# Six probability tiles, a split of the row maxima over two engines, and new instruction lists in an attention block

## What is computed

```python
x = x + _layernorm(_L0_attn_ref(_layernorm(x), W_qkv, b_qkv, W_out, b_out))
x = x + _layernorm(_L0_ffn_ref(_layernorm(x), weight, alpha, bias))
# _L0_attn_ref: 16 heads of 8, 4 groups of keys and values
qkv = x @ W_qkv + b_qkv
scores = einsum('bkgsd,bktd->bkgst', q, k) / sqrt(8)
attn = softmax(where(causal, scores, -inf))
y = einsum('bkgst,bktd->bkgsd', attn, v)
return y @ W_out + b_out
# _L0_ffn_ref: weights become +1, 0, -1 by 0.7 * mean(|w|), times alpha, plus bias
```

## Time and profile before

| | us |
|---|---|
| median of 3 runs (lowest, highest) | 456.02 (455.45, 457.24) |
| the profiled execution | 456.64 |
| its span, first to last instruction | 454.8 |
| busy: TensorE / VectorE / ScalarE / GpSimd | 398.6 / 394.7 / 333.3 / 296.3 |
| TensorE weight loads busy | 280.8 |

### The profile page before, as it was taken

The page is one execution under the profiler, slowest core; times in us unless marked ns, Lnnn a source line. Parts: engine busy times, 40 slices in busy tenths (PEclk is TensorE's granted clock), DMA queues, the critical chain, the costliest instruction groups (busy, mean ns, idle before and its releaser), DMA issues.

```text
span 454.8 us, 19223 instructions
## 1 busy us (share of the span) xinstructions
PE 398.6 (88%) x7430; PEld 280.8 (62%) x7430; DVE 394.7 (87%) x1180; ACT 333.3 (73%) x609; POOL 296.3 (65%) x552
## 2 busy tenths in 40 slices
PE   0569999999999999999999999999999999998551
PEld 0336766676666676666666666676676777764330
DVE  5957878999999999999999999999999989995442
ACT  0333877777888888888888888888888888888332
POOL 2622323657677877777777777787777666766676
PEclk9999999999999999999999999999999999999855
DMA  7176465524434344444344444443444543421342
GB/s 190 35 121 94 103 107 133 127 75 85 77 72 80 81 76 81 78 76 79 66 70 77 76 72 80 81 75 80 82 74 85 114 84 69 87 77 30 111 145 73
DMA packets 72307, 39.59 MB, mean 87 GB/s; under 512 B 13048, under 2 KB 68056, under 8 KB 72216
## 3 DMA queue, kind: packets, MB, share of 16 engines
q1 hardware_dynamic: 70880, 37.70, 41.7%
q10 hardware_dynamic: 1336, 0.66, 0.5%
HBM read 13.67 MB, written 4.72 MB: 40 GB/s over the span
## 4 chain that ended last, share of the span: by engine, by line
PE 47%; DVE 29%; issue 9%; DMA 4%; POOL 3%; SPq 3%; ACT 2%; POOLq 0%; DVEq 0%; ACTq 0%
DVE M L619 13%; PE ps_mx L843 13%; PE ps_y L816 11%; PE ps_w L872 7%; PE ps_st L792 7%; PE ps_w L913 5%; DVE stats L584 4%; DVE xn L602 3%; DMA QS<-part 3%; DVE A L666 2%; DVE mv L594 2%; PE ps_w L893 2%; DVE Mp L683 2%; DVE F L674 2%; SPq L260 2%
## 5 line engine op out<-in xcount | busy, mean ns | idle before, releaser
L619 DVE TENSOR_REDUCE M<-ps_mx 128x2 f32<-128x512 f32 (+3 forms) x352 | 210.5, 626 | 14.2 <-PE ps_mx L843 13.5
L419 ACT ACTIVATE PT<-ps_st 128x1024 f32<-128x1024 f32 (+1 forms) x192 | 165.3, 884 | 20.4 <-PE ps_st L792 20.3
L843 PE MATMUL ps_mx<-KS,QS 112*64 112x128 bf16 (+2 forms) x2560 | 132.7, 228 | 15.9 <-DVE M L619 11.6
L843 PEld LDWEIGHTS ps_mx<-KS,QS 112*64 112x64 bf16 x2560 | 89.6, 112 | 60.9 <-DVE M L619 37.2
L358 POOL TENSOR_TENSOR rstd<-vareps,mhalf 128x2 f32<-128x2 f32 x128 | 93.0, 727 | 10.0
L792 PE MATMUL ps_st<-QS,KS 114*64 114x256 bf16 (+1 forms) x1024 | 97.9, 300 | 0.2 <-DMA QS<-MpT 0.2
L816 PE MATMUL ps_y<-PT,VB 128*32 128x256 f32 (+3 forms) x2048 | 90.4, 304 | 1.3 <-ACT PT L419 1.0
L356 POOL TENSOR_TENSOR vareps<-mv,eps 128x2 f32<-128x2 f32 x128 | 25.9, 203 | 73.3 <-DVE mv L594 73.3
L816 PEld LDWEIGHTS ps_y<-PT,VB 128*32 128x32 f32 x2048 | 46.7, 109 | 28.6 <-issue 9.4
L393 POOL TENSOR_TENSOR rest<-QK,part 128x512 f32<-128x512 f32 x32 | 38.2, 1193 | 24.3 <-ACT part L448 24.1
L792 PEld LDWEIGHTS ps_st<-QS,KS 114*64 114x64 bf16 x1024 | 52.0, 111 | 1.5 <-DMA QS<-MpT 0.5
(11 more groups left out here) (63 smaller groups left out, 512.9 us busy)
## 6 DMA issues: line engine op xcount, KB each, us to landing
QS<-part SPq DMA_DIRECT2D x192, 64.0 KB
rden<-rec_dram SPq DMA_DIRECT2D x32, 256.0 KB
X<-in_x SPq DMA_DIRECT2D x7, 512.0 KB, 6.3
out<-X SPq DMA_DIRECT2D x7, 512.0 KB, 5.4
KS<-part SPq DMA_DIRECT2D x32, 96.0 KB
KS<-part SPq DMA_DIRECT2D x32, 64.0 KB
KS<-part SPq DMA_DIRECT2D x32, 32.0 KB
QS<-MpT SPq DMA_DIRECT2D x32, 16.0 KB
```

Source lines behind the costliest of these rows:

```text
L419: nc.scalar.activation(PT[(b * CHUNKS + n) % TILES][:, 0:512 * banks], ps_st[n % 2][:, 0:banks, :].rearrange("p a c -> p (a c)"), ACT.Exp, ...
L619: nc.vector.tensor_reduce(M[b % 2][:].rearrange("p k g i -> p (k g) i")[:, 2 * kv:2 * kv + pairs, i], ps_mx[(b * BANKS + n) % 2][:, 0:pair ...
L843: last = pe.matmul(ps_mx[(b * BANKS + n) % 2][64 * one:64 * one + 64, at:at + w], q[:, h, BL * i:BL * i + BL], k[:, kv, blocks, :], start= ...
```

## The change

Three things. TILES goes from 3 to 6, so that exp waits for pv of six chunks earlier. `split_max` becomes `high_max`, a single tensor_reduce over an axis of length one that turns M into its high bf16 part, and `low_max` on GpSimd subtracts it from M; the turn waits for both as before. And every list is written in another order, with other distances between the stages: op stands five steps after x1, not six, and the nine stack transfers of a batch are spread over two steps of SP. The lists that run before the loops (on TensorE and VectorE) are changed to match; they are left out below.

```diff
 BANKS = 11
-TILES = 3
+TILES = 6
...
                 load_x(t)
+                spread_rec(t - 5)
+                send_max(t - 3)
+                q_rows(t - 1, 1, 1)
+                q_rows(t - 1, 1, 5)
+                k_rows(t - 1, 2)
+                q_rows(t - 1, 2, 0)
+                store_x(t - 21)
+                send_den(t - 4)
                 rows_free(t)
-                k_rows(t, 0)
+                q_rows(t, 0, 2)
                 q_rows(t, 0, 3)
                 q_rows(t, 0, 4)
-                store_x(t - 25)
+                store_rec(t - 4)
+                k_rows(t, 0)
                 k_rows(t, 1)
-                send_max(t - 2)
-                q_rows(t, 1, 1)
...
                     gp.tensor_tensor(yn[i][:], Y[i][:], rden[i][:], ALU.mult).then_inc(s_yn, 1)
 
+            def low_max(b):
+                if on(b):
+
+                    gp.wait_ge(s_mp, 2 * b + 1)
+                    gp.tensor_tensor(Mp[:, 1, :], M[b % 2][:].rearrange("p k g i -> p (k g i)"), Mp[:, 0, :],
+                                     ALU.subtract).then_inc(s_mp, 1)
...
 
             def step(t):
-                add_normed(t - 10, A2, s_a2, s_x1)
-                third(t - 4)
                 inverse(t, 0)
-                divide(t - 9)
-                inverse(t - 10, 2)
-                inverse(t - 12, 3)
-                inverse(t - 9, 1)
+                divide(t - 8)
                 remainder(t - 3)
-                add_normed(t - 13, F2, s_f2, s_fin)
-
-            for t in range(B + 13):
+                inverse(t - 9, 2)
+                add_normed(t - 12, F2, s_f2, s_fin)
+                low_max(t - 5)
+                inverse(t - 8, 1)
+                third(t - 3)
+                inverse(t - 10, 3)
+                add_normed(t - 8, A2, s_a2, s_x1)
+
+            for t in range(B + 12):
...
             def step(t):
-                take_v(t - 1)
-                exp(t - 4, 3)
-                take_turned(t - 3)
                 take_xn1(t)
-                exp(t - 4, 4)
                 exp(t - 4, 5)
                 take_qk(t)
+                take_y(t - 4)
+                take_xn3(t - 7)
                 first_part(t)
-                take_y(t - 4)
-                norm(t - 10, 3, F1, F2, s_f2, s_fin)
                 exp(t - 3, 0)
+                take_v(t)
                 exp(t - 3, 1)
-                norm(t - 6, 1, A1, A2, s_a2, s_x1)
-                take_xn3(t - 7)
                 exp(t - 3, 2)
+                norm(t - 8, 3, F1, F2, s_f2, s_fin)
                 second_part(t)
-
-            for t in range(B + 10):
+                exp(t - 3, 3)
+                exp(t - 3, 4)
+                take_turned(t - 2)
+                norm(t - 5, 1, A1, A2, s_a2, s_x1)
+
...
@@ -674,15 +682,13 @@
                     nc.vector.tensor_tensor(F1[b % 2][:], ps_w[:, 0:S].rearrange("p (j d) -> p j d", j=TT),
                                             bf_sb[:], ALU.add).then_inc(s_f1, 1)
 
-            def split_max(b):
-                if on(b):
-                    m = M[b % 2][:].rearrange("p k g i -> p (k g i)")
+            def high_max(b):
+                if on(b):
 
                     dve.wait_ge(s_mx, BANKS * b + BANKS)
                     free(dve, b, s_mt_ps)
-                    nc.vector.tensor_tensor(Mp[:, 0, :], m, m, ALU.max).then_inc(s_mp, 1)
-                    dve.wait_ge(s_mp, 2 * b + 1)
-                    nc.vector.tensor_tensor(Mp[:, 1, :], m, Mp[:, 0, :], ALU.subtract).then_inc(s_mp, 1)
+                    nc.vector.tensor_reduce(Mp[:, 0, :], M[b % 2][:].rearrange("p k g i -> p (k g i)").unsqueeze(2), AX_X,
+                                            ALU.max).then_inc(s_mp, 1)
 
...
 
             def step(t):
-                invert_den(t - 10)
-                maxima(t - 7, 4)
-                spread_x1(t - 12)
-                moments(t - 12, 2)
-                moments(t - 14, 3)
-                maxima(t - 7, 5)
-                maxima(t - 7, 6)
-                take_a(t - 11)
-                spread_a(t - 11)
-                moments(t - 11, 1)
-                maxima(t - 7, 7)
-                take_f(t - 13)
-                norm_x1(t - 12)
-                maxima(t - 7, 8)
-                maxima(t - 7, 9)
-                maxima(t - 7, 10)
-                split_max(t - 7)
-                moments(t - 1, 0)
+                maxima(t - 6, 2)
+                norm_x1(t - 11)
+                maxima(t - 6, 3)
+                maxima(t - 6, 4)
+                spread_x1(t - 10)
+                maxima(t - 6, 5)
+                maxima(t - 6, 6)
+                maxima(t - 6, 7)
+                moments(t - 10, 2)
+                maxima(t - 6, 8)
+                maxima(t - 6, 9)
+                invert_den(t - 8)
+                take_a(t - 9)
+                maxima(t - 6, 10)
+                spread_a(t - 9)
+                high_max(t - 6)
+                moments(t - 9, 1)
+                take_f(t - 11)
                 spread_x(t)
-                maxima(t - 6, 0)
-                maxima(t - 6, 1)
-                spread_f(t - 13)
-                maxima(t - 6, 2)
-                norm_x(t - 2)
-                maxima(t - 6, 3)
+                spread_f(t - 11)
+                moments(t, 0)
+                maxima(t - 5, 0)
+                maxima(t - 5, 1)
+                norm_x(t - 1)
...
 
             def step(t):
-                st(t - 4, 4)
+                ff(t - 8)
+                mx(t - 2, 1)
+                pv(t - 4, 0)
+                turn(t - 3)
+                pv(t - 4, 1)
+                pv(t - 4, 2)
+                pv(t - 4, 3)
                 x1(t)
+                mx(t - 2, 2)
+                st(t - 4, 5)
                 mx(t - 2, 3)
-                st(t - 4, 5)
+                qk(t)
                 mx(t - 2, 4)
-                qk(t)
-                mx(t - 2, 5)
-                pv(t - 4, 3)
                 pv(t - 4, 4)
                 pv(t - 4, 5)
+                x3(t - 7)
+                mx(t - 2, 5)
+                st(t - 3, 0)
                 mx(t - 2, 6)
-                op(t - 6)
-                st(t - 3, 0)
+                v(t)
                 mx(t - 2, 7)
-                ff(t - 8)
                 st(t - 3, 1)
                 mx(t - 2, 8)
+                st(t - 3, 2)
                 mx(t - 2, 9)
-                pv(t - 3, 0)
-                x3(t - 7)
+                op(t - 5)
                 mx(t - 2, 10)
-                st(t - 3, 2)
                 st(t - 3, 3)
-                v(t)
                 mx(t - 1, 0)
-                mx(t - 1, 1)
-                pv(t - 3, 1)
-                pv(t - 3, 2)
-                turn(t - 2)
-                mx(t - 1, 2)
+                st(t - 3, 4)
 
...
```

More of the change, by code:

```diff
@@ L961, in _ @@
             v(0)
+            x1(1)
             constants()
-            for t in range(1, B + 8):
+            qk(1)
+            v(1)
+            mx(0, 0)
+            for t in range(2, B + 8):
                 step(t)
```

28 lines of the change are left out of this document (10 added, 18 removed).

## The result

The changed kernel took **448.36 us** (median of four runs: 442.58, 445.44, 451.27, 456.03), the kernel before 456.12 beside it (455.45 to 457.24). So it is faster, by 2 to 3%, where 6% were forecast, and 448.36 lies outside 415 to 447. The profiled execution is the fastest of the four, 442.58 us with a span of 440.8; even that is 13 us above the forecast.

The account below looks back on a forecast made before the run. It took a loop over VectorE and TensorE to bound the kernel at 12.36 us a period. Periods -20.8, outer ones -1.5, tail -5.5, head +1 made -26.8 from 456.64, so 429.8, forecast as 429 us, range 415 to 447.

Parts of the forecast that it names:

- The head: Start of the run: SP issues the second 512 KB load of X earlier; cost 0 to 3 us, 1 taken.
- The period: Time per batch in the middle: from 12.25 to 11.45 us, ends 11.05 and 11.9, saving 20.8 over 26 periods.
- the forecast's loops: Middle: each ps_mx bank followed round VectorE and TensorE in the new lists; each loop gives between 10.2 and 11.0 us.
- the engines' own sums: Middle: work per period of VectorE, 11.15 us, and TensorE, 11.3; no loop was said to hold more.
- The tail: After the last Mp: one turn of 7.7 us falls away, 2 taken off for batch 31; saves 5.5, ends 0 and 7.7.
- The high part: VectorE's one remaining Mp instruction: 0.25 us, bounded by 0.19 and 0.42; saving 0.8 us per period with the pair replaced.
- The low part: Subtraction moved to GpSimd: 0.26 us for 128x32, ends 0.20 and 0.73, with room in GpSimd's busy time.
- cover of 0.5 us: Middle: time to spare before TensorE's turn would wait for GpSimd's low part, 0.5 us or so.
- Six tiles: ScalarE's exp waits for P·V of six chunks before; the tiles by themselves worth 0 to 0.16 us a period.
- Denominator round trip: Rival, 0.07: den transfer and reciprocal return late to VectorE; with 2 us late, period 12.7 to 13, total 466.
- Port lock: Rival, 0.06: GpSimd's low part and a VectorE norm hold each other up over SBUF ports; about 437 us.
- TensorE's real time: Rival, 0.17: TensorE's list really costs 11.9 us a period, so the loops gain only 0.35; total 445.

Follow-up runs that it names:

- kernel with the loads late: Changed kernel with the first load of X unmoved and the six later ones at the end of SP's steps 2, 6, ... 22: 445.53 us.
- maxima first: Changed kernel with send_max(t-3) ahead of spread_rec(t-5) in SP's list, nothing else: 470.01 us, ratio 1.0271.
- three Y tiles: Changed kernel with a third Y tile, divide and all behind it one step later, maxima ahead of SP's spread, reciprocal behind the last maximum: 455.37 us.
- store later: Changed kernel with three Y tiles, divide onward one step later, late loads, and SP storing the reciprocals one step later, spread behind the last stack transfer: 461.68 us.

## Why the prediction was wrong

**The head (+1 forecast, +9.9 measured).** This is the term that failed. It saw the right edit, the load of X now ahead of the last four stack transfers, and had its price, 6.3 us to land. Then it let it count once, as 0 to 3, since "the stack of batch 1 lies behind the same load in both orders". But several loads follow each other in the head, each ahead of transfers for which mx waits; batch 0's Mp loses only the forecast 1.0, and the next four periods lose 8.9, where the sum had them gain 1.7. The kernel with the loads late has Mp of batch 4 9.6 us earlier. With this term right, the sum for the profiled execution would have been about 440 and not 430. That is inside the range; that the median lies outside it takes, besides, the 5.8 us between the profiled execution and the median, whose cause is open.

**The period (11.45 forecast, 11.41 measured).** Right as an average, and for a reason only half right. The loads' wait for M fell from 25.6 to 7.0 us, "under 12" as forecast. But the period does not rest on the low part's move to GpSimd: with it back on VectorE the time is the same. Undisturbed the lists reach 10.7, within the 10.2 to 11.0 of the forecast's loops but below the engines' own sums, 11.15 and 11.3, which it took as the floor. Their average is 0.7 above 10.7; the longest period holds a late MpT, and no term had such stops. So the forecast took too high a floor and left the stops out, and that this came to 11.45 beside 11.41 is luck. Where the split does count is in the old lists, and there it needs the norm's move.

**The tail (-5.5 forecast, -4.0 measured).** Three takes of A, as forecast; the last stands 3.63 us for op.

**The small costs.** The high part took 0.168 us; I had taken 0.25, above the early row's 0.19. The rule of the Trainium skill ("SBUF — State Buffer", Who interferes with whom) that I weighed there, that tensor_reduce never contends, was the better guide: 0.19, and no instance took more. The low part: 0.245 against 0.26. Its cover of 0.5 us was too small: TensorE's loads waited for it 11 times, 5.5 us in 300. Six tiles: nothing, within 0 to 0.16.

**The rivals.** *Denominator round trip:* its waits are there (6.6 us on VectorE, 4.7 on GpSimd of 300) and it did not decide, at 0.3 of 11.4 us. Its price for the landing, 1.5 to 2.1, was too low: where den is in the chain of the changed kernel between 59 and 384 us it took 2.9 to 4.9. I looked for it in a single loop. What the trace has is a family: MpT, den, rec, the spread and the stacks share SP's queue, and each came late in some kernel. Three kernels, maxima first, three Y tiles and store later, each freed one and met the next. *Port lock:* not in the change (the low part never went above 248 ns, norms take 352 on average against the 420 of the earlier trace rows), but it ruled the old lists with the split alone. *TensorE's real time:* 445 for it is nearer to the result than the forecast is, by accident: its 11.9 us did not occur, the head did.

**What stays open.** Why runs of the one changed kernel spread from 442.58 to 456.03, where the kernel before stays within 2 us beside it. It is not the clock: the mean granted clock of the slowest was 0.953, that of the 445.44 run the same. The number of late transfers is the likely cause, but only the fastest run has a trace; that is argued, not shown. Nor is it shown how the head's loss divides into landing and half clock. The granted clock reads 0.50 from 41.3 to 47 us, where the kernel before reads 1.00 from 36 to 46, and yet eight matmuls of mx take 1.07 us in both (at 41.30, and at 38.04 before); so the two heads can't be compared by that number.

**A better version.** The old lists with the split and the norm later: 442.57, all four runs within 3.0 us. Its ratio's interval overlaps that of the change (0.9630 to 0.9723, and 0.9687 to 0.9762); against the median of the change it is 5.8 us faster, and the change equals it only in its fastest run. It varied less; that it is faster is not shown.

## What to carry to other kernels

When a list of instructions is tightened, price the transfers by the worst landing in the trace and not by the usual one, and look in the issuing queue for what goes out shortly ahead of each: here the small transfers among large ones were those that came late. In a pipeline's head, where steps are short and loads follow each other closely, count a large load once for each step that has urgent transfers behind it. When an engine is relieved and nothing is gained, look at which of its instructions became longer; two instructions that now meet another engine's long one can cost more than was saved.

## What the runs showed of the hardware

- A transfer of 16 KB issued 0.7 us behind one of 256 KB took 5.51 and 4.04 us (den), and 5.53 when issued 3.5 us behind one with stack transfers between. MpT behind such a spread took 4.2 until st started; sent from ScalarE 5.30 and 5.78. The shortest landing of a 16 KB transfer (rec) was 1.5. Which of the large transfers is the cause is not shown; no run takes one away.
- Of two VectorE normalisations of 0.34 us, the second stood 1.03 us for a GpSimd multiply of 1.28 us; moved away from it, the mean was 339 ns instead of 574.
- A tensor_reduce over an axis of one, 128x32, took 168 ns in the new lists and 186 in the old; the subtraction on GpSimd 245 and 247.
- A stop of 1.57 us in full work was followed by 1.2 us at 1.00 of the clock and 3.4 us at 0.50; one of 1.88 us by 8 us at 1.00, and in the kernel with the loads late one of 2.46 us (ended at 281.96) by 8 us at 1.00.
